# One merged stage order for the feed forward part, and a few cross attention stages at other places

## What is computed

```
x = layernorm(x + attention(x))      # 16 heads, 64 memory slots a head (ABC attention), gated, times Wo
x = layernorm(x + cross(x, ctx))     # q, k from ctx (256 wide); softmax(q k^T); x times its transpose, over the 512 columns of x
x = layernorm(x + ffn(x))            # I = 2048
ffn:  gate, up = bitlinear(x, w_gate), bitlinear(x, w_up)
      h = silu(gate) * up
      bitlinear(fwht(h), w_down)     # fwht: Walsh-Hadamard transform over the 2048 columns
bitlinear(x, w): x rounded to 8 bits with one scale for each row, w rounded to -1, 0, 1
```

## Time and profile before

| | us |
|---|---|
| median of 3 runs | 1571.05 (1569.86 to 1573.0) |
| the profiled execution | 1571.14 |
| its span in the trace | 1569.2 |
| TensorE busy | 1520.3 (97%) |
| VectorE busy | 1043.4 (66%) |
| ScalarE busy | 652.4 (42%) |
| GpSimd busy | 433.7 (28%) |

### The profile page before, as it was taken

How to read it: one execution, slowest core, us unless ns; L and a number is a source line. 1 busy time by engine, 2 the same in 40 slices (tenths; PEclk the granted TensorE clock), 3 DMA queues, 4 the chain that set the end, 5 groups by cost and what they waited for, 6 DMA issues and landing times.

```text
span 1569.2 us, 24173 instructions
## 1 busy us (share of the span) xinstructions
PE 1520.3 (97%) x9570; PEld 1203.8 (77%) x9570; DVE 1043.4 (66%) x1988; ACT 652.4 (42%) x1245; POOL 433.7 (28%) x282
## 2 busy tenths in 40 slices
PE   6999999999999999999999999999999799999996
PEld 5888888888888888888788888877878656666664
DVE  4556665565556666655666577686787976787786
ACT  4333333333323333333434334324333355867664
POOL 1111011110214344434454323221331234333310
PEclk9999999999999999999999999999999989999999
DMA  7112111120202122222232201101210413544551
GB/s 261 63 37 75 44 48 55 54 68 28 74 1 88 58 78 67 75 68 68 81 101 88 81 28 48 61 8 34 61 55 12 150 47 108 155 128 143 154 175 61
DMA packets 107552, 121.17 MB, mean 77 GB/s; under 512 B 5296, under 2 KB 75056, under 8 KB 107312
## 3 DMA queue, kind: packets, MB, share of 16 engines
q1 hardware_dynamic: 103984, 113.33, 23.0%
q10 hardware_dynamic: 3456, 6.29, 1.1%
HBM read 92.34 MB, written 27.26 MB: 76 GB/s over the span
## 4 chain that ended last, share of the span: by engine, by line
PE 85%; DVE 7%; issue 3%; DMA 2%; ACT 1%; POOL 1%; SPq 0%; POOLq 0%; DVEq 0%; ACTq 0%
PE bank L438 18%; PE bank L440 16%; PE bank L439 16%; PE bank L649 6%; PE bank L547 3%; PE bank L664 3%; PE bank L685 3%; PE bank L483 2%; PE bank L533 2%; PE bank L509 2%; PE bank L555 2%; PE bank L492 2%; PE bank L497 2%; PE bank L504 1%; PE bank L541 1%
## 5 line engine op out<-in xcount | busy, mean ns | idle before, releaser
L438 PE MATMUL bank<-Wh,X 128*128 128x512 f32 x512 | 211.0, 412 | 1.1 <-DVE Y L1086 1.1
L440 PE MATMUL bank<-Wh,X 128*128 128x512 f32 x512 | 200.8, 392 | 0.0
L439 PE MATMUL bank<-Wl,X 128*128 128x512 f32 x512 | 200.0, 391 | 0.0
L776 ACT ACTIVATE V<-bank 128x256 f32<-128x256 f32 x128 | 49.2, 384 | 324.1 <-PE bank L440 324.1
L438 PE MATMUL bank<-X,Wh 128*128 128x512 f32 x384 | 161.2, 420 | 12.3 <-DVE X L957 12.3
L1344 POOL TENSOR_TENSOR sm<-sm,half 128x8 f32<-128x8 f32 x32 | 52.8, 1650 | 396.5 <-DVE sm L1062 396.4
L1326 POOL TENSOR_TENSOR Wl<-RAW,Wh 128x512 fp32r<-128x512 f32 (+1 forms) x65 | 112.8, 1744 | 143.5 <-ACT Wh L731 143.5
L440 PE MATMUL bank<-X,Wl 128*128 128x512 f32 x384 | 151.3, 394 | 0.0
L439 PE MATMUL bank<-X,Wh 128*128 128x512 f32 x384 | 150.0, 391 | 0.0
L649 PE MATMUL bank<-XT,W 128*128 128x512 bf16 x512 | 123.5, 386 | 2.2 <-DVE M L1215 2.0
L1367 POOL TENSOR_TENSOR LO<-M,HI 128x512 fp32r<-128x512 f32 x64 | 82.0, 1281 | 152.1 <-PE bank L658 127.7
(11 more groups left out here) (190 smaller groups left out, 3252.5 us busy)
## 6 DMA issues: line engine op xcount, KB each, us to landing
z_scratch<-EV SPq DMA_DIRECT2D x64, 256.0 KB, 2.3
Z<-z_scratch SPq DMA_DIRECT2D x16, 1024.0 KB, 6.0
RAW<-wgT SPq DMA_DIRECT2D x16, 512.0 KB, 3.8
RAW<-wuT SPq DMA_DIRECT2D x16, 512.0 KB, 3.9
RAW<-wdT SPq DMA_DIRECT2D x16, 512.0 KB, 3.6
RAW<-Wo SPq DMA_DIRECT2D x14, 512.0 KB, 3.7
RAW<-Wv SPq DMA_DIRECT2D x26, 256.0 KB, 2.9
RAW<-Wg SPq DMA_DIRECT2D x26, 256.0 KB, 3.2
```

The costliest lines, as they stand in the source:

```text
L438: engine.matmul(o, lh(c), rh(c), start=c == 0, stop=False)
L439: engine.matmul(o, lh(c), rl(c), start=False, stop=False)
L440: last = engine.matmul(o, ll(c), rh(c), start=False, stop=c == n - 1)
L776: engine.activation(V[:, par, i, :], bk[:, 0:256], ACT.Copy).then_inc(S["v_evac"], 1)
```

## The change

Four tables and the functions that read them change; no instruction is added or removed, and each keeps its operands apart from the PSUM bank that it uses.

- `SEAM`: values 31 stands one place later.
- `PLACES`, b = 0: qk one place later, x101 and x123 and their copies three later (x123 is now behind energy), x_made0, x_round1, x_made1, x_turned and x_turned_out one later (x_turned now stands behind q 29, not keys 28). b = 2: ctx two places earlier, n1 one earlier, so that VectorE applies the norm ahead of its work for values 29.
- `UNIT` and `TILE` become one list, all offsets in units. Within a unit TensorE now does had1 and turn_q ahead of had2; VectorE does absmax, clamp and turn_q_out ahead of h and gs, then scale, add and normal; add and normal stand one unit later, SyncE's out store three later.
- `HOLD`: seven of the numbers change.

```diff
--- before.py
+++ after.py
@@ -111,7 +111,7 @@
 
 
 SEAM = (("keys", 31), ("scores", 31), ("states", 31), ("turn_o", 30), ("ok", 31), ("y", 30), ("turn_ok", 31), None,
-        None, None, ("turn_w", 31), None, ("weights", 31), ("values", 31), None, None, ("turn_o", 31), ("unit", 0),
+        None, None, ("turn_w", 31), None, ("weights", 31), None, ("values", 31), None, ("turn_o", 31), ("unit", 0),
         ("unit", 1), ("unit", 2), ("unit", 3), ("y", 31))
 SEAM_UNITS = 4
 IN_SEAM = len(PLACED) * (STEPS - 1)
@@ -130,15 +130,15 @@
 
 
 PLACES = (
-    dict(ctx=400, centre=403, n1=406, qk=407, qk_out=409, x101=411, x101_out=412, x123=416, x123_out=417,
-         energy=418, energy_out=419, att_scale=419, att01=422, att01_out=423, att23=424, att23_out=426, xm0=430,
-         xm0_out=431, xm1=433, xm1_out=434, xm2=435, xm2_out=436, xm3=438, xm3_out=439, x_round0=440, x_made0=442,
-         x_round1=442, x_made1=444, x_turned=448, x_turned_out=449),
+    dict(ctx=400, centre=403, n1=406, qk=408, qk_out=409, x101=414, x101_out=415, energy=418, x123=419,
+         energy_out=419, att_scale=419, x123_out=420, att01=422, att01_out=423, att23=424, att23_out=426, xm0=430,
+         xm0_out=431, xm1=433, xm1_out=434, xm2=435, xm2_out=436, xm3=438, xm3_out=439, x_round0=440, x_made0=443,
+         x_round1=443, x_made1=445, x_turned=449, x_turned_out=450),
     dict(ctx=445, centre=445, qk=447, qk_out=448, n1=449, x101=450, energy=451, x101_out=452, energy_out=452,
          x123=454, att_scale=454, x123_out=455, att01=456, att01_out=457, att23=457, att23_out=458, xm0=459,
          xm0_out=461, xm1=463, xm1_out=464, xm2=464, xm2_out=465, xm3=465, xm3_out=466, x_round0=467, x_made0=468,
          x_round1=468, x_made1=471, x_turned=475, x_turned_out=476),
-    dict(centre=476, ctx=477, n1=478, qk=479, qk_out=480, x101=481, x101_out=482, energy=483, energy_out=484,
+    dict(ctx=475, centre=476, n1=477, qk=479, qk_out=480, x101=481, x101_out=482, energy=483, energy_out=484,
          x123=486, att_scale=486, x123_out=487, att01=488, att01_out=489, att23=489, att23_out=490, xm0=492,
          xm0_out=493, xm1=494, xm1_out=495, xm2=496, xm2_out=497, xm3=498, xm3_out=499, x_round0=500, x_made0=501,
          x_round1=501, x_made1=503, x_turned=504, x_turned_out=505),
@@ -167,46 +167,39 @@
 
 
 
-UNIT = (("gate", 0), ("h", 1), ("absmax", 25), ("had1_out", 5), ("gs", 0), ("high", 2), ("low", 2), ("had2", 23),
-        ("had1", 4), ("had2_out", 24))
-
-TILE = (("round", 6), ("clamp", 7), ("turn_q_out", 9), ("add", 11), ("normal", 12), ("store", 12), ("scale", 5),
-        ("turn_q", 8), ("down", 10))
-
-
-LAG = 23
-
-HOLD = (("o", 11), ("en", 8), ("y", 8), ("vg", 8), ("xm", 7), ("gate", 6), ("up", 8), ("h1", 6), ("h2", 8), ("down",
-        8), ("hq", 8), ("xt", 9), ("q", 5), ("k", 5), ("s", 5), ("sc", 8), ("wt", 8), ("ok", 12), ("okt", 8), ("w",
-        8), ("ot", 8), ("kt", 7), ("et", 8), ("hk", 9), ("hv", 8), ("att", 9), ("x1", 9), ("qk", 9), ("spread", 8))
+
+UNIT = (("absmax", 25), ("had1_out", 5), ("clamp", 30), ("turn_q_out", 32), ("high", 2), ("low", 2), ("gate", 0),
+        ("h", 1), ("had1", 4), ("had2_out", 24), ("read", 20), ("round", 29), ("gs", 0), ("scale", 28), ("add", 35),
+        ("normal", 36), ("store", 38), ("turn_q", 31), ("had2", 23), ("down", 33), ("silu", 0))
+TILES = {"read", "scale", "round", "clamp", "turn_q_out", "add", "normal", "store", "turn_q", "down"}
+
+
+
+HOLD = (("o", 11), ("en", 8), ("y", 8), ("vg", 8), ("xm", 7), ("gate", 6), ("up", 6), ("h1", 6), ("h2", 8), ("down",
+        8), ("hq", 8), ("xt", 9), ("q", 5), ("k", 5), ("s", 5), ("sc", 8), ("wt", 8), ("ok", 12), ("okt", 7), ("w",
+        8), ("ot", 8), ("kt", 7), ("et", 8), ("hk", 6), ("hv", 5), ("att", 10), ("x1", 9), ("qk", 8), ("spread", 8))
 
 
 def ffn_place(n):
 
 
     for stage, off in UNIT:
-        if 0 <= n - off < 64:
+        if stage in TILES:
+            i, rest = divmod(n - off, 4)
+            if rest == 0 and 0 <= i < 16:
+                yield stage, i
+        elif 0 <= n - off < 64:
             yield stage, n - off
-    i, rest = divmod(n - 20, 4)
-    if rest == 0 and 0 <= i < 16:
-        yield "read", i
-    for stage, off in TILE:
-        i, rest = divmod(n - LAG - off, 4)
-        if rest == 0 and 0 <= i < 16:
-            yield stage, i
-    if n < 64:
-        yield "silu", n
     if n >= SEAM_UNITS:
         yield from beside(IN_UNITS + n - SEAM_UNITS)
 
 
 def ffn_order():
-    for n in range(SEAM_UNITS, 60 + LAG + 13):
+    for n in range(SEAM_UNITS, 61 + max(off for _, off in UNIT)):
         yield from ffn_place(n)
 
 
-FEED = {"gate", "h", "gs", "silu", "high", "low", "had1", "had1_out", "had2", "had2_out", "absmax", "read", "turn_q", "down",
-        *(stage for stage, _ in TILE)}
+FEED = {stage for stage, _ in UNIT}
 
 
 SEMAPHORES = """
```

## The result

The changed kernel takes 1557.13 us (median of 6 runs, 1554.21 to 1558.07) beside 1570.45 for the kernel before in the same sessions (6 runs, 1565.85 to 1574.92). The ratio is 0.9911, with a 95% interval of 0.9896 to 0.9926: 14.0 us, give or take 2.4. Forecast were 1560.3 and a range of 1553.5 to 1566.5. The profiled execution took 1557.25 us, with a span of 1555.1.

A forecast was written before the change was run, and what follows sets the result against it. TensorE was taken as full in the steady parts, losing time only in cross attention, seam and tail; -0.4 - 2.5 - 2.2 - 1.9 - 3.8 = -10.8 took 1571.1 to 1560.3 us, range 1553.5 to 1566.5.

The forecast's parts named there:

- The total: Whole kernel: the terms sum to -10.8 us, from 1571.1 to 1560.3 us.
- The bound: TensorE is full in steady attention and feed forward; only cross attention, seam and tail lose time that order can gain.
- the prediction's own signs of being wrong: Steady-part gaps of had1 or gate on L1215, longer waits 1200 to 1260, old read waits, half clock at new places.
- Bank numbers: Most bank takes get another bank; in the steady attention no new last use is later than its take: 0.
- Cross attention 0, first half: Waits of turn_ok (0.7) and weights 25 (0.5) go, new late banks cost some 0.8: -0.4, between -1.2 and +0.4.
- Cross attention 0, second half: values 27 0, qk 1 -1.0, x_turned 0 -1.7, half clock -1.0, late banks +1.2: -2.5, between -4 and 0.
- Cross attention 2: x101 2's wait for n1 goes, -1.4, and qk 2's wait, -0.8: -2.2, between -2.6 and 0.
- First rival: Cross attention 3 gives the 5.1 us of cross attention gains back as longer gaps: 1565.4 us, chance 0.14.
- Tail, reads: Reads issued ahead of out stores: three waits (0.9) and 1.0 of 2.1 go: -1.9, between -0.9 and -3.0.
- second rival: Tail reads limited by how long 1 MB takes, lower clock stays, only 2.0 gained there: 1564.0 us, chance 0.16.
- Tail, last tiles: down 14's wait -1.0, its half clock -1.7, down 15's wait -1.1: -3.8, between -1.0 and -4.5.
- Third rival: Steady feed forward: clamp or normal beside GpSimd's low delays h, had1 waits 1.2 per cycle: 1575.9 us, slower, chance 0.06.

The follow-up runs named there:

- e3: The new HOLD bank numbers alone, put in the kernel before: 1568.78 us, ratio 0.9983 to before.
- e8: The changed kernel with add and normal one unit earlier and ahead of h: 1562.92 us, ratio 0.9947 to before.
- e6: The changed kernel with x_made0, x_round1 and x_made1 of cross attention 0 back at their old places: 1555.21 us, ratio 0.9899 to before.
- e5: The changed kernel with GpSimd's low half of Wo of step 26 held until VectorE has made cross attention 0's second-half scales: 1555.07 us, ratio 0.9901 to before.
- e1: The new PLACES and SEAM alone, put in the kernel before: 1567.59 us, ratio 0.9978 to before.
- e7: The changed kernel with the out store two units earlier, right ahead of the read on SyncE's queue: 1563.83 us, ratio 0.9952 to before.
- e9: The changed kernel with TensorE's had2 ahead of had1 and turn_q again: 1558.45 us, ratio 0.9904 to before.
- e11: e10 with GpSimd's context low half (cross attention 3) and last Wo low half held for x_round0's scales and x_made1: 1551.03 us, ratio 0.9874 to before.
- e10: e6 with cross attention 3's ctx one place earlier and GpSimd's last Wo low half held for cross attention 2's scales: 1555.08 us, ratio 0.9885 to before.
- e4: The changed kernel with the old HOLD bank numbers: 1559.99 us, ratio 0.9932 to before.

## Why the prediction was right, and where not

*The total* hides what its terms missed. The gain was 3.2 more than forecast: the reads gave 2.2 more and the seam 1.3 that no term had, against 1.5 less in the second half of cross attention 0. The seam's 1.3 is luck. The prediction looked at two low stretches of the kernel before and gave those from 1233.90, 1254.38 and 1288.52 on no term; and the one at turn_o 31 is long, short or absent behind the same wait (last section).

*The bound* was right but for one wait: the steady attention is as full as before, the feed forward part but for the 0.63 at 1337.01, and the gain came from cross attention, seam and tail. That wait for h and the low stretch at 1052.47 are two of the prediction's own signs of being wrong. The first is small; the second stands at the step that failed.

*Bank numbers* were called 0; e3 shows 0.17%. The step is not far off, but it followed the takes of the steady attention, and the waits that the numbers change stand beside cross attention 3.

*Cross attention 0, first half*: 0.8 instead of 0.4, within its bounds. turn_ok's and weights 25's waits went as forecast, and the new ones cost less than the 0.8 set against them.

*Cross attention 0, second half*: the step that failed. "values 27 needs masks from the same queue of VectorE and inherits it: 0" held for the order of the queue and not for the durations in it. With the x stages behind the y adds, x_limit falls beside GpSimd's Wo and takes 1.6 us more, so values 27 waits 2.8 and not some 1.1, and TensorE runs at 0.50 behind that wait, which by e8 costs only 0.3 of the stretch. Of the 2.5 forecast 1.0 came; e6 shows the other end, with 1.8 more. The other terms were right in kind: qk 1 waits no longer, and x_turned 0 behind q 29 has neither wait nor low clock, at the price of 0.7 at x101 1, where 1.2 had been set. The half clock that went with the gap had been set at 1.0; e3, with the gap and without the low clock, shows 1.6. That x_turned 0 has no wait at all is luck: TensorE comes late to it, and where it does not, in e5 and e8, the wait is 1.0, and not the 0.5 of the sum.

*Cross attention 2*: 2.6 instead of 2.2, by both terms: neither qk 2 nor x101 2 waits, and n1 takes 1.91 for four where it took 3.99.

```profile
1155.65 1.91 DVE L1092 TENSOR_SCALAR Y<-Y,mv,rs 128x512 f32<-128x512 f32 x4
```

*First rival*: the gains were not given back in cross attention 3; at its end the changed kernel is more than 5 us ahead, and e1 has its 4.7 there too.

*Tail, reads*: right in mechanism, the size off. "three waits (0.9) go" and "1.0 of 2.1 goes" gave 1.9; 4.1 came: all four waits (3.0) went, the one for read 12 too, of which only half had been counted, and each had cost some 0.16 more than the time listed: the long one, 2.08, lies between two starts that are 3.14 apart and 0.9 without a wait. Some 0.4 stay open. e7 shows that the store's place alone costs 5.9, with normal as late as it is now; e9 shows that had1's place adds to it, as argued, with 1.3 for read 12. The second rival (1 MB reads that are late whenever they are issued) falls with that.

*Tail, last tiles*: 3.9 against 3.8: waits of 1.48 and 1.79 against 2.68 and 2.98, and down 14 in 3.61 at full clock. e8 gives the 4.1 back with add and normal alone.

*Third rival*: VectorE's clamp does fall beside GpSimd's low, and is longer: 1.64 for the pair in the changed kernel (VectorE and GpSimd, a steady cycle) where two of 0.69 overlap to 1.28.

```profile
1445.19 1.64 DVE L1243 TENSOR_SCALAR HQ<-H 128x1024 bf16<-128x1024 f32 x2
...
1444.39 1.28 POOL L1360 TENSOR_TENSOR LO<-M,HI 128x512 fp32r<-128x512 f32 x1 [1.79 <-PE bank L651]
```

0.36 is no 1.0, nothing waits for h there, and the steady part gained 0.3. The mechanism was real and stood at another place: in the forecast it was put to the clamp, where it costs nothing, and not to the small scales of cross attention, where it cost 1.6. The rule of the Trainium skill, SBUF — State Buffer, "Who interferes with whom", covers both: it lists tensor_scalar among the operations that can take the shared port pair. The traces agree, with 1.78 against 0.17 for the same instruction in the changed kernel and in e5.

## What to carry to other kernels

When stages are put in a new order, don't check only what stands ahead of what in each queue: check which VectorE instructions will run beside a long GpSimd instruction, however small they are. In these runs the small tensor_scalar instructions between SBUF tiles that started beside one took as long as the rest of the large one. In a DMA queue that serves loads and stores, a store that waits for the last result stands best behind the loads that the next work needs. And a gain is best read at the start of the same stage in two traces, as a single low clock stretch can move whole times by more than a wait of a microsecond; take off what the two traces differ by ahead of the stretch.

## What the hardware showed that was not expected

*Small tensor_scalar instructions of VectorE are held back whole.* Two numbers a partition took 1.78, 1.80 and 2.24 us instead of about 0.2 beside a GpSimd instruction of 2.35 to 2.42 us, and ended with it; with GpSimd held back the 1.78 and the 2.24 were 0.17 and 0.21 (e5, e11). A reciprocal of the same size was not: in e10 L1172 took 0.17 at 1221.43, when GpSimd's had been running since 1221.31.

```profile
1221.43 0.17 DVE L1172 RECIPROCAL ax<-ax 128x2 f32<-128x2 f32 x1
```

*The clock is not lowered behind every gap of a length.* In e3 x_turned 0 waits 2.19 us as before, and the clock stays at its upper level behind it, where before it fell to the lower:

```profile
1061.71 1.05 PE L629 MATMUL bank<-IDB,XI 128*128 128x128 bf16 x16 [2.19 <-issue]
```

```profile
1062.50:1066.00 3.50, 3.50 (x24) 3.10 (x22) 3.07 (x6) 0.00 (x0) 0.00 (x0) 1.00 0.00 0
```

From x_turned 0 to the end of q 29 takes 4.7 us in e3 and 6.3 before, with no change of a wait. turn_o 31 waits 3.22 in all thirteen traces: the low clock around it lasts 6.8 us in four of them (before, e1, e3, e9), 3.4 in seven, and doesn't come in two (e4, e8). So part of the differences between kernels of this size, and the seam's 1.3 in the result, is which gaps a low clock falls on.
